# A two-layer graph kernel whose loops over pairs of chunks become straight sequences of chunks

## The reference, cut to what matters

```python
h = relu(layernorm(x))                      # x: (8192, 128) float32
wh = h @ W                                  # layer 0
e = wh @ a[:128] + (wh @ a[128:]).T         # 8192 x 8192
e = where(e > 0, e, 0.2 * e); e = where(adj > 0, e, -9e15)
x = x + elu(softmax(e, axis=-1) @ wh)
h = relu(layernorm(x))                      # layer 1
Qn, Kn = cos_normalize(h @ Wq.T), cos_normalize(h @ Wk.T)
att = softmax(where(adj > 0, Kn @ Qn.T, -9e15), axis=1)
prop = att @ h                              # rows without neighbours keep h
x = x + 0.5 * prop + 0.5 * h
```

## Time and profile before

| | |
|---|---|
| median of three runs | 2272.36 us |
| profiled execution | 2268.91 us |
| span in the profile | 2267.0 us |
| mean granted clock of TensorE | 0.989 |
| TensorE matmuls busy | 2189.4 us, 97% |
| VectorE busy | 1981.7 us, 87% |
| ScalarE busy | 1635.2 us, 72% |
| adjacency loads | 512 of 1 MB |

### The profile page before, as it was taken

One profiled execution on the slowest core, in us unless ns is written; L12 is line 12 of the kernel. 1 busy time (PEld: TensorE's weight loads), 2 busy tenths in 40 slices (PEclk: granted clock), 3 DMA queues, 4 the chain that ended last, 5 costly groups with the idle time before them and its releaser, 6 DMA issues.

```text
span 2267.0 us, 69253 instructions
## 1 busy us (share of the span) xinstructions
PE 2189.4 (97%) x28293; PEld 1801.9 (79%) x28293; DVE 1981.7 (87%) x1685; ACT 1635.2 (72%) x1423; POOL 1.4 (0%) x9
## 2 busy tenths in 40 slices
PE   5999999999999988999999999999999999999999
PEld 4999999999999966777677677677767767767777
DVE  7999989998999889888788888888878888888887
ACT  5787777776777667777677677677767767767776
POOL 0000000000000000000000000000000000000000
PEclk9999999999999999999999999999999999999999
DMA  6899999998999924565565565655656656655653
GB/s 246 319 361 397 384 390 370 380 408 339 393 397 373 381 65 149 194 210 205 190 210 204 200 207 197 218 191 199 215 177 209 218 177 209 218 186 206 212 203 113
DMA packets 153497, 573.55 MB, mean 253 GB/s; under 512 B 9888, under 2 KB 10336, under 8 KB 152928
## 3 DMA queue, kind: packets, MB, share of 16 engines
q1 hardware_dynamic: 144096, 549.78, 67.0%
q10 hardware_dynamic: 9216, 20.98, 2.4%
HBM read 558.11 MB, written 12.62 MB: 252 GB/s over the span
## 4 chain that ended last, share of the span: by engine, by line
PE 85%; DVE 6%; issue 6%; ACT 1%; DMA 1%; DVEq 0%; ACTq 0%; POOL 0%; POOLq 0%; SPq 0%
PE bank L1068 31%; PE bank L1051 29%; PE bank L984 24%; DVE ring L780 4%; DMA ring<-adj 1%; DVE hl_buf L805 0%; PE bank L1001 0%; PE bank L1012 0%; DVE norm L794 0%; ACT ring L463 0%; DVE v_buf L812 0%; DVE stats L741 0%; ACT hl_buf L439 0%; DVE q_buf L812 0%; ACT ring L527 0%
## 5 line engine op out<-in xcount | busy, mean ns | idle before, releaser
L527 ACT ACTIVATE ring<-bank 128x1024 f32<-128x1024 f32 x512 | 523.8, 1023 | 384.1 <-PE bank L1051 383.9
L1068 PEld LDWEIGHTS bank<-u_buf,hl_buf 128*128 128x128 f16 x12288 | 721.9, 97 | 60.4 <-issue 0.6
L838 DVE SCALAR_TENSOR_TENSOR ring<-ring 128x2048 f32<-128x2048 int32 x256 | 586.8, 2292 | 202.3 <-ACT ring L527 202.3
L1068 PE MATMUL bank<-u_buf,hl_buf 128*128 (+2 forms) x12288 | 742.6, 220 | 0.2 <-DVE hl_buf L843 0.2
L984 PE MATMUL bank<-v_buf,ring 128*128 128x129 f16 (+1 forms) x12288 | 717.0, 220 | 17.0 <-DVE ring L780 13.8
L1051 PE MATMUL bank<-v_buf,q_buf 128*128 (+1 forms) x3072 | 710.4, 381 | 21.2 <-issue 18.9
L984 PEld LDWEIGHTS bank<-v_buf,ring 128*128 128x128 f16 x12288 | 711.9, 98 | 21.9 <-issue 15.9
L780 DVE SCALAR_TENSOR_TENSOR ring<-r_ring,th_word,ring 128x1024 f32<-128x1024 f32 x512 | 621.9, 1287 | 39.9 <-ACT ring L463 36.6
L843 DVE TENSOR_TENSOR hl_buf<-ring,hl_buf 128x2048 f16<-128x2048 f32 x256 | 584.7, 2284 | 0.0
L463 ACT ACTIVATE ring<-ring 128x2048 f32<-128x2048 int32 x256 | 484.1, 1912 | 132.1 <-DMA ring<-adj 128.3
L1051 PEld LDWEIGHTS bank<-v_buf,q_buf 128*128 (+1 forms) x3072 | 291.6, 98 | 328.6 <-issue 28.9
(11 more groups left out here) (102 smaller groups left out, 417.8 us busy)
## 6 DMA issues: line engine op xcount, KB each, us to landing
ring<-adj SPq DMA_DIRECT2D x512, 1024.0 KB, 5.6
r_ring<-a_rows SPq DMA_DIRECT2D x8, 512.0 KB, 6.4
x_dram<-q_buf ACTq DMA_DIRECT2D x8, 512.0 KB, 7.6
h_dram<-hl_buf ACTq DMA_DIRECT2D x8, 512.0 KB, 6.9
hl_buf<-h_dram SPq DMA_DIRECT2D x16, 256.0 KB, 2.7
r_ring<-x_dram ACTq DMA_DIRECT2D x16, 256.0 KB, 3.7
r_ring<-h_dram ACTq DMA_DIRECT2D x16, 256.0 KB, 3.9
out<-r_ring ACTq DMA_DIRECT2D x16, 256.0 KB, 3.7
```

The source lines that it names most:

```text
L527: nc.scalar.activation(p_ring[:, k, hf * 1024:(hf + 1) * 1024], bank[:, 2 * hf:2 * hf + 2, :].rearrange("p b n -> p (b n)"), ACT.Exp, scal ...
L838: V.scalar_tensor_tensor(p_ring[:, k, :], adj_ring[:, k, :], 0.0, p_ring[:, k, :], ALU.is_gt, ALU.mult).then_inc(s_m, 1)
L1068: ins = mm(o, hl_buf[:, ps, k, f], v.rearrange("p o c -> p (o c)"), start=head and m == 0 and it % 2 == 0 and (ps, us) == (0, 0), stop=tai ...
```

## The change

`chunks0` and `chunks1` become Python loops: each chunk is written out with a constant number, on all four engines. The parity of a chunk is the same as before. The short `Fori` loops within a chunk stay. The order of the work on each engine is not changed, nor are tiles, buffers, waits or loads. TensorE's stream then holds 8 chunks of layer 0 and 16 of layer 1, where it held 4 and 4.

```diff
-        def chunks0(eng, chunk):
-            chunk(0, 0)
-            with eng.Fori(0, (NC0 - 2) // 2) as pair:
-                chunk(2 * pair + 1, 1)
-                chunk(2 * pair + 2, 0)
-            chunk(NC0 - 1, 1)
+        def chunks0(chunk):
+            for c in range(NC0):
+                chunk(c, c % 2)
 
-        def chunks1(eng, chunk):
-            chunk(0, 0)
-            with eng.Fori(0, (NI - 2) // 2) as pair:
-                chunk(2 * pair + 1, 1)
-                chunk(2 * pair + 2, 0)
-            chunk(NI - 1, 1)
+        def chunks1(chunk):
+            for i in range(NI):
+                chunk(i, i % 2)
...
-            chunks0(pe, chunk)
+            chunks0(chunk)
...
-            chunks1(pe, chunk1)
+            chunks1(chunk1)
```

## The result

The changed kernel takes 2231.56 us (median of four runs, 2230.49 to 2231.89), against 2268.34 us for the kernel before beside it (2263.53 to 2272.42). The ratio is 0.9838, with a 95% interval of 0.9812 to 0.9864: 1.6% faster. The prediction was 2232 us with a range of 2224 to 2246. Its profiled execution took 2231.89 us, with a span of 2230.0 us and a mean clock of 0.996; before it was 2268.91, 2267.0 and 0.989.

The account below looks back on a forecast made before the run. TensorE was taken to bound both layers, losing time at its pair loops' far jumps back. From 2268.91 us, 25.68 (layer 1) and 11.47 (layer 0) were taken off, other terms 0: 2231.8, forecast 2232 us, range 2224 to 2246.

Parts of the forecast that it names:

- Step 1: Layer 1: six far jumps of TensorE go, with slow clock behind some; 25.7 us gained, bounds 18.9 and 25.7.
- Step 2: Layer 0: two far jumps of TensorE go, 11.47 us gained; new waits for VectorE 0, at most 3 us.
- Step 3: All four engines: waits and addresses counted from the pair's register become constants; taken as 0, between 0 and 80 us.
- Step 4: ScalarE, layer 0: table loads move to line 423, just as many; cost taken as 0, upper end 3.8 us.
- Step 5: SyncE's issues keep number and order, its far jump costs 50 ns or less; 1.9 us around the span stays.
- Step 6: More code: TensorE's fetches hardly change, VectorE and ScalarE have time for new code; taken as 0, at most 5.8 us.
- A: Rival: layer 0 gives nothing, being bound elsewhere by DMA or VectorE; 2243 us, chance 0.10.
- B: Rival: first pass over new code stops TensorE, or the branch only shows other time; no change, 2268 us, chance 0.06.
- C: Rival: short loops at 24 places, some near jumps become far at 4.6 us each; slower, 2296 us, chance 0.04.

Follow-up runs that it names:

- run 7: Kernel before, pair loops kept, with a hint instruction naming the closing branch in TensorE's pair loops only: 2241.01 us, ratio 0.9869.
- run 9: Changed kernel with 700 waits added in TensorE's short loop of layer 0, its body grown from 810 to 1510 instructions: 3468.48 us.
- run 10: Changed kernel with 1400 waits added in TensorE's short loop of layer 0, its body grown to 2210 instructions: 4718.50 us.
- run 2: Kernel before with VectorE, ScalarE and SyncE written out in both layers while TensorE keeps its pair loops: 2268.15 us, ratio 0.9993.
- run 1: Kernel before with only TensorE's chunks written out; VectorE, ScalarE and SyncE keep both pair loops: 2233.92 us, ratio 0.9855.
- run 6: Changed kernel with TensorE's short loops within the chunks of both layers written out too: 2231.71 us, ratio 0.9827 to the kernel before.
- run 3: Kernel before with layer 0 written out on all engines, layer 1 keeping its pair loop: 2256.84 us, ratio 0.9952.
- run 4: Kernel before with layer 1 written out on all engines, layer 0 keeping its pair loop: 2240.38 us, ratio 0.9885.
- run 5: Changed kernel with layer 1 on all engines as a loop of three turns of four chunks, other chunks straight: 2241.10 us, ratio 0.9874.
- run 11: Kernel before with the hint in all engines' pair loops and TensorE's layer 0 loop starting at slot 50 of its block: 2236.28 us, ratio 0.9856.

## Why the prediction was right

The number came out for the reason given: the loss was read from the turns, and it sat at TensorE's jumps. The sum doesn't depend on why a far jump stops TensorE, though. That its code has to be fetched was an untested reading in the prediction, and runs 7, 9 and 10 are what supports it.

**What bounds the kernel.** Right. TensorE is busy through every inner chunk at clock 1.00, and the two best chunks of before were the measure of all chunks after.

**Step 1, layer 1.** Forecast 25.68 us, measured 25.71 us by windows. The slow clock behind the stops was counted in and went with them, so the upper bound was the right value. That the clock falls after 3 us without matmuls holds for three of the six stops only; the other three kept 1.00. Run 2 shows that nothing else in the change touches it.

**Step 2, layer 0.** Forecast 11.47 us, measured 11.45 us. The claim that the branch and not VectorE held TensorE at 518 us is shown by runs 1 and 2 from both sides. VectorE's lead did stay positive, with no wait in the layer behind the first chunk. The price of losing it was put at 3 us at most and was slightly too low: run 1, where VectorE keeps its stops, has 3.3 us by the windows (1.2 and 2.1), 2.3 of them as waits.

**Step 3, register work.** Taken at 0, and 0 it is. But little of TensorE's went at the line that the forecast names: 1536 of its 1564 instructions are left, since the short loops within a chunk still count in a register.

```profile
L1045 PEldq FUSED_REGOPS  x1536: 46/55/89, 872.6 to 2210.7; - x192
```

That register work costs nothing is shown by other runs: run 2 takes it away on three engines, with a ratio of 0.9993, and run 6, where none of it is left on TensorE in the two layers, takes the time of the changed kernel.

**Step 4, table loads.** The cost of 0 was right, the count was wrong: six stand at the line, not seven. The first of the three at the head of the loop (143.5 us before) went altogether; my reading is that the loop's body, which stands once, had to load the table for every turn, and the straight first turn doesn't need it.

**Step 5, SyncE and the rest.** Right: 2231.89 - 2230.0 = 1.9 us lie around the span, as before.

**Step 6, more code.** Right in cost. That what TensorE must fetch hardly changes was wrong: 141 fetches instead of 156. Fewer jumps mean fewer fetches throughout: 152 in run 3 with six far jumps, 145 in runs 4 and 5 with two.

**The sum.** 2231.8 us against 2231.89 for the profiled execution. The choice not to add the 3.4 us between profile and median was right. The median of the runs of before fell to 2268.3 with the next one, which was the scatter that the jumps bring.

**The rivals.** A is out by the windows of after, B by run 6, C by the short loops' branches of 233 ns at most and by runs 9 and 10. The compare-and-branch of about 108 ns in the Trainium skill ("Advanced Engine Details and Errata", Control Flow Timing) lies between what the trace has for a near jump on TensorE, 208 ns, and for any jump on VectorE, 50 to 67 ns, and is off by a factor of 30 for TensorE's far ones. The skill's "Runtime: NRT & Kernel Launch", section Instruction fetch mechanics, has the rule that fits: a taken branch whose target isn't in the current window of code has to wait for a fetch of the target. Runs 7, 9 and 10 agree with it, and the 2048 instructions that it gives TensorE's instruction memory lie within the 1510 to 2110 found here. Its window of two blocks of 256 doesn't fit TensorE: loops of 560 and 810 instructions jumped back in 233 ns at most.

## What to carry to other kernels

Look at the loop's own line in the profile: a compare-and-branch of microseconds on the bounding engine is a stop at every turn, and it appears elsewhere only as "issue" or, wrongly, as a wait for another engine. On TensorE write such a loop out or keep its body below what was cheap here, 1510 instructions with weight loads and matmuls counted apart; a hint for the branch does nearly as well, but where the branch stands matters: at about the 235th place of its block of 256 it worked, at about the 19th it didn't. On an engine that runs ahead, the same stop costs nothing until it uses up the lead, so look again after the first one is gone.

## What the runs showed of the hardware

- The branch of a far jump of TensorE takes 3.4 to 3.9 us in layer 1 and 4.2 to 6.1 us in layer 0, where the DMA share is 1.01. In run 10, also layer 0, the share is 0.22 between 100 and 1000 us and the branch takes 3.3 to 3.8 us, so the full DMA engines are the likely reason for the longer ones. Twice the distance takes the same time. The matmuls stand still for less than the branch takes: about 3.2 us in layer 1, 2.7 and 4.3 us in layer 0 before.
- The slow clock behind a stop isn't certain: three of the six stops of layer 1 before had it within 5 us, three not, for stops of the same length. It makes the time scatter: 15 runs of the kernel before, taken beside runs 1 to 4, spread over 2263.7 to 2276.6 us, four of the changed one over 1.4 us. Run 7, whose stops of layer 1 are gone, spreads over 1.2 us.
- The hint costs 36 to 50 ns on TensorE and shortens a far jump from 3557 to 360 ns; where its branch falls through, TensorE stopped for 2.0 us in layer 0 of run 11 and not at all in layer 1.
